# Context loaded a second time in transposed layout, mLSTM values shifted on GpSimd instead of centred on TensorE, router matmuls moved in the step

## The reference

```python
x = x + wkv(w, u, k=layernorm(x), v=ctx)          # a decaying running average of ctx, per channel over time
x = x + attention(layernorm(x))                   # 16 heads of 32
x = x + mlstm(q=layernorm(x), k=ctx, v=ctx)       # 16 heads of 32
x = x + moe(layernorm(x))                         # 32 experts, the best 8 of each token, limited capacity

# in mlstm: ig, fg = [q, k, v] @ Wi, [q, k, v] @ Wf;  D = decay matrix of the gates
Cn = (q @ k.T / sqrt(dh)) * D / normalizer
h  = Cn @ v
hn = (h - h.mean(-1)) * rsqrt(h.var(-1) + eps)    # per head, so a shift of v that is equal over a head's channels drops out
# in moe: probs = softmax(x @ gate_w); top 8; each (expert, token) pair gets a slot while the expert has room
```

## Time and profile before

| what | value |
|---|---|
| time, median of 3 runs | 2157.45 us (2155.42 to 2159.64) |
| profiled execution, first to last instruction | 2155.5 us |
| time of the profiled execution itself | not given apart from the three runs |
| TensorE matmuls busy | 1944.1 us, 90% of the span |
| VectorE busy | 1582.7 us, 73% |
| ScalarE busy | 1203.0 us, 56% |
| GpSimd busy | 1575.2 us, 73% |
| mean granted TensorE clock | 0.977 of full speed |
| first part (pipeline of sequences) | to about 1085 us |

### The profile page before, as it was taken

How to read it: one execution, slowest core, us unless ns; L and a number is a source line. 1 busy time by engine, 2 the same in 40 slices (tenths; PEclk the granted TensorE clock), 3 DMA queues, 4 the chain that set the end, 5 groups by cost and what they waited for, 6 DMA issues and landing times. The chain is left out here.

```text
span 2155.5 us, 66447 instructions
## 1 busy us (share of the span) xinstructions
PE 1944.1 (90%) x22263; PEld 1463.4 (68%) x22296; DVE 1582.7 (73%) x3230; ACT 1203.0 (56%) x3018; POOL 1575.2 (73%) x1776
## 2 busy tenths in 40 slices
PE   0799999999999999997259999999999999999997
PEld 0677667777667766675146777777777777777775
DVE  5688888888888888985236676777766667767664
ACT  3466666666666666665135555555554555545553
POOL 6336778777777777876667777777767777777775
PEclk9999999999999999999579999999999999999999
DMA  3111110111101111101048888777788888887876
GB/s 108 38 34 37 40 39 30 34 34 40 39 29 34 34 39 39 32 27 43 16 111 172 186 193 160 176 181 171 167 178 186 170 178 182 169 190 156 184 153 103
DMA packets 141452, 222.72 MB, mean 103 GB/s; under 512 B 32944, under 2 KB 65840, under 8 KB 141360
## 3 DMA queue, kind: packets, MB, share of 16 engines
q0 software_dynamic: 74752, 144.02, 33.9%
q1 hardware_dynamic: 62000, 69.24, 10.4%
q10 hardware_dynamic: 4608, 8.39, 1.0%
HBM read 136.34 MB, written 96.73 MB: 108 GB/s over the span
## 5 line engine op out<-in xcount | busy, mean ns | idle before, releaser
L2162 POOL DMA_INDIRECT out_dram<-y,m_add x300 | 498.1, 1660 | 171.0 <-POOLq L2170 112.5
L2288 PE MATMUL ps<-xh,wh 128*128 128x256 f16 x1752 | 398.3, 273 | 4.7 <-PEq L2300 4.7
L2289 PE MATMUL ps<-xh,wl 128*128 128x256 f16 x1752 | 398.3, 273 | 0.0
L2154 POOL DMA_INDIRECT xg<-z_scratch,slot_t x292 | 295.8, 1013 | 96.4 <-issue 83.4
L630 POOL DMA_INDIRECT slot_scratch<-pair,slots x256 | 304.8, 1191 | 70.2 <-issue 58.1
L2365 ACT ACTIVATE y<-ps,wts_now 128x512 f32<-128x512 f32 x294 | 185.2, 681 | 143.4 <-ACTq L2364 143.4
L2293 PE MATMUL ps<-xl,wh 128*128 128x256 f16 x1752 | 239.0, 273 | 1.3 <-PEq L2304 1.3
L2439 DVE SCALAR_TENSOR_TENSOR hx<-ps,s 64x256 f16<-64x256 f32 x146 | 62.2, 426 | 216.3 <-DVEq L2462 215.6
L2381 ACT ACTIVATE xh<-ps 128x512 f16<-128x512 f32 x146 | 87.2, 597 | 224.0 <-ACTq L2380 224.0
L2288 PEld LDWEIGHTS ps<-xh,wh 128*128 128x128 f16 x1752 | 171.3, 98 | 45.9 <-issue 12.8
L2289 PEld LDWEIGHTS ps<-xh,wl 128*128 128x128 f16 x1752 | 171.4, 98 | 33.1
(11 more groups left out here) (345 smaller groups left out, 5001.4 us busy)
## 6 DMA issues: line engine op xcount, KB each, us to landing
wst<-in_L_ffn_w_gate_dram SPq DMA_DIRECT2D x32, 384.0 KB
wst<-in_L_ffn_w_up_dram SPq DMA_DIRECT2D x32, 384.0 KB
xt<-in_x_dram SPq DMA_DIRECT2D x32, 256.0 KB
ct<-in_ctx_dram SPq DMA_DIRECT2D x32, 256.0 KB, 2.6
out_dram<-x SPq DMA_DIRECT2D x32, 256.0 KB, 2.1
z_scratch<-zn ACTq DMA_DIRECT2D x32, 256.0 KB, 2.0
wdst<-in_L_ffn_w_down_dram SPq DMA_DIRECT2D x32, 256.0 KB
out_dram<-y,m_add POOLq DMA_INDIRECT x300, 5.1
```

Of the source, the lines that this page charges most:

```text
L2154: pool.indirect_dma_start(out=xg[b][:, h, :], out_offset=None, in_=z_d[:, :], in_offset=bass.IndirectOffsetOnAxis(ap=rows(h), axis=0)).the ...
L2162: pool.indirect_dma_start(out=acc_d[:, :], out_offset=bass.IndirectOffsetOnAxis(ap=m_add[:, k, h:h + 1], axis=0), in_=y[:, k, h, :], in_of ...
L2288: pe.matmul(ps[:, dst, 0:GROUP], wh[:, j, k, c0:c0 + P], xh[:, k, :], start=(k == 0), stop=False)
L2289: pe.matmul(ps[:, dst, 0:GROUP], wl[:, j, k, c0:c0 + P], xh[:, k, :], start=False, stop=False)
```

## The change

The host lays the context out a second time, transposed (`ctx_cols`, channels on partitions). SyncE now makes three context loads per step: `vT` from `ctx_cols` for wkv, `kT2` from `ctx_cols` two steps later for the mLSTM key, and `ct` as before, for the mLSTM values. `ctx_turn`, `vT_copy`, `hold_ctx`, `spread_ctx`, `centre` and `centred_copy` are gone. The values are made by GpSimd from `ct` as each head's 31 columns minus the head's last column (`values`); `bmat` is changed so that `heads_back` takes the mean off and rebuilds the last column. On TensorE `router` moves from behind `heads_back` to ahead of `head_sums`, with its result in another PSUM bank. On VectorE three small operations are written as `scalar_tensor_tensor` with two inputs from SBUF (`stabiliser_floor`, `choose`, `take_places`), and the f32 copy `sel` of the choice is dropped.

```diff
+                def load_own_cols(i):
+                    sp.wait_ge(own_cols_free, 1)
+                    sp.sem_inc(own_cols_free, -1)
+                    sp.dma_start(vT[:, :, :], ctx_cols[bass.ds(i, 1)].rearrange("a p k t -> p (a k) t")).then_inc(own_cols_loaded, 16)
...
                 with sp.Fori(3, nb - 1) as i:
-                    load_ctx(i + 1)
+                    load_key_cols(i - 2)
+                    load_ctx(i - 1)
+                    load_own_cols(i + 1)
                     store(i - 3)
                     load_x(i + 1)
...
-                def spread_ctx():
-                    return pool.tensor_copy(kT2[:, :, :], vTk[:, :, :])
-
-                def hold_ctx():
-                    return pool.tensor_copy(vTk[:, :, :], vT[:, :, :])
+                def values():
+                    heads = ct[:, :].rearrange("p (h d) -> p h d", h=H)
+                    return pool.tensor_tensor(vc[:, :, 0:DH - 1], heads[:, :, 0:DH - 1],
+                                              heads[:, :, DH - 1:DH].to_broadcast([P, H, DH - 1]), ALU.subtract)
...
                         weigh_cc().then_inc(weigh_cc_ready, 1)
                         weigh_gg().then_inc(weigh_gg_ready, 1)
+                    if on(3):
+                        pool.wait_ge(values_free, 1)
+                        pool.sem_inc(values_free, -1)
+                    if on(2):
+                        pool.wait_ge(ctx_loaded, 16)
+                        pool.sem_inc(ctx_loaded, -16)
+                        values().then_inc(values_done, 1)
                     if on(5):
                         pool.wait_ge(pool_step, 1)
                         pool.sem_inc(pool_step, -1)
                         store_pair(3)
                         store_pair(2)
...
-                    if on(0):
-                        vT_copy().then_inc(vT_copy_ready, 1)
...
-                        act.wait_ge(centre_ps, 1)
-                        act.sem_inc(centre_ps, -1)
-                        centred_copy()
...
-                    if on(0):
-                        pe.wait_ge(ctx_loaded, 16)
-                        pe.sem_inc(ctx_loaded, -16)
-                        ctx_turn().then_inc(ctx_turn_ps, 1)
-                    if on(3):
+                    if on(4):
+                        pe.wait_ge(zT_copy_ready, 1)
+                        pe.sem_inc(zT_copy_ready, -1)
+                        router().then_inc(router_ps, 1)
+                    if on(3):
+                        pe.wait_ge(values_ready, 1)
+                        pe.sem_inc(values_ready, -1)
                         pe.wait_ge(decayed_scores0_ready, 1)
                         pe.sem_inc(decayed_scores0_ready, -1)
                         head_sums().then_inc(head_sums_ps, 1)
...
-                    if on(4):
-                        router().then_inc(router_ps, 1)
...
-                        centre().then_inc(centre_ps, 1)
...
-                    return dve.tensor_scalar(fm[:, :], fm[:, :], -50.0, None, ALU.max)
+                    return dve.scalar_tensor_tensor(fm[:, :], fm[:, :], -50.0, fm[:, :], ALU.max, ALU.max)
...
-                    dve.tensor_scalar(sel[:, :], er2[:, :], 0.0, None, ALU.is_lt)
-                    return dve.tensor_scalar(selb[:, :], er2[:, :], 0.0, None, ALU.is_lt)
+                    return dve.scalar_tensor_tensor(selb[:, :], er2[:, :], 0.0, onesf[:, 0:E], ALU.is_lt, ALU.mult)
...
-                    return dve.tensor_tensor(selacc[:, :], selacc[:, :], selb[:, :], ALU.add)
+                    return dve.scalar_tensor_tensor(selacc[:, :], selacc[:, :], 1.0, selb[:, :], ALU.mult, ALU.add)
```

More of the change, by code:

```diff
@@ L255, in build @@
             ctx_loaded = once("ctx_loaded")
+            own_cols_loaded = once("own_cols_loaded")
+            key_cols_loaded = once("key_cols_loaded")
+            own_cols_free = once("own_cols_free")
+            key_cols_free = once("key_cols_free")
+            ctx_free = once("ctx_free")
+            values_free = once("values_free")
+            values_ready = once("values_ready")
+            values_done = once("values_done")
             scratch_set = once("scratch_set")
@@ L504, in _ @@
                   .then_inc(scratch_set, 16)
-                for i in range(1, 3):
-                    load_ctx(i + 1)
-                    load_x(i + 1)
+                load_ctx(0, first=True)
+                load_own_cols(2)
+                load_x(2)
+                load_key_cols(0, first=True)
+                load_ctx(1)
+                load_own_cols(3)
+                load_x(3)
                 with sp.Fori(3, nb - 1) as i:
-                    load_ctx(i + 1)
+                    load_key_cols(i - 2)
+                    load_ctx(i - 1)
+                    load_own_cols(i + 1)
                     store(i - 3)
                     load_x(i + 1)
-                sp.wait_ge(ctx_turn_ps, 1)
-                sp.sem_inc(ctx_turn_ps, -1)
+                load_key_cols(nb - 3)
+                load_ctx(nb - 2)
+                sp.wait_ge(own_cols_free, 1)
+                sp.sem_inc(own_cols_free, -1)
                 store(nb - 4)
@@ L517, in _ @@
                 sp.sem_inc(first_residual_ready_for_sp, -1)
+                load_key_cols(nb - 2)
+                load_ctx(nb - 1)
+                store(nb - 3)
+                load_key_cols(nb - 1)
                 load_weights(sp, 0)
-                for i in range(nb - 3, nb):
+                for i in range(nb - 2, nb):
                     store(i)
@@ L558, in spreads @@
                         put(pick[q_, :, :], 1.0, 0, [[-1, 4], [0, P]])
-                        put(bmat[q_, r, 0:DH - 1], 1.0, 0, [[-1, DH - 1]])
+                        done(pool.memset(bmat[q_, r, 0:DH], -1.0 / DH))
+                        put(bmat[q_, r, 0:DH - 1], 1.0 - 1.0 / DH, 0, [[-1, DH - 1]])
+                        put(bmat[q_, r, 0:DH], 0.0, 1 - DH, [[0, DH]])
                         put(bmat[q_, r, DH:DH + 1], 1.0, 1 - DH, [[0, 1]])
-                        done(pool.memset(bmat[q_, r, DH - 1:DH], -1.0))
-                        put(bmat[q_, r, DH - 1:DH], 0.0, 1 - DH, [[0, 1]])
-                        done(pool.memset(cmat[q_, 32 * r:32 * r + DH - 1], -1.0 / DH))
                 def first_constants():
@@ L715, in step @@
                         pool.sem_inc(qk_ps_for_dve, 1)
[L716 to L724, removed]
+                        pool.sem_inc(key_cols_free, 1)
                     if on(5):
@@ L1250, in project @@
                     return m
-                def ctx_turn():
-                    return turn(CT_BANK, lambda c: ct[:, c * P:(c + 1) * P])
                 def head_sums():
@@ L1304, in gates @@
                                           start=(j == 0), stop=(j == 1))
-                    return m
-                def centre():
-                    for c in range(4):
-                        m = pe.matmul(ps[:, VC_BANK, c * P:(c + 1) * P], kT2[:, c, :], cmat[:, :], start=True, stop=True)
                     return m
@@ L2494, with give @@
     arrays, args = {}, []
-    for name in _INS:
-        a = _np.ascontiguousarray(inputs[name])
+    def give(name, a):
+        a = _np.ascontiguousarray(a)
         arrays[f"in_{name}_dram"] = a
         args.append(nc.dram_tensor(f"in_{name}_dram", a.shape, _mybir.dt.from_np(a.dtype), kind="ExternalInput").ap())
+    for name in _INS:
+        give(name, inputs[name])
+        if name == 'ctx_2048':
+            rows = inputs[name].shape[1]
+            give('ctx_columns', inputs[name].reshape(-1, rows, 4, 128).transpose(0, 3, 2, 1))
     out = nc.dram_tensor("out_0_dram", (32, 128, 512), _mybir.dt.float32, kind="ExternalOutput").ap()
```

65 lines of the change are left out of this document (25 added, 40 removed).

## The result

The changed kernel takes 2196.99 us (median of 4 runs, 2195.15 to 2199.57) against 2157.81 us of the kernel before in the same runs (2155.42 to 2159.64): ratio 1.0184, 95% interval 1.0172 to 1.0195. It is slower by 39.2 us. The forecast was 2184 with a range of 2146 to 2207 and slower as the likeliest sign.

What follows compares the result with a forecast made beforehand. The prediction took a chain through GpSimd, not TensorE, to bound the kernel. Its terms 0.28 + 1.15 - 0.45 = +0.98 us a step over 27 steps gave +26.5 us on 2157.45: 2184 us, range 2146 to 2207.

Steps and rivals of the forecast that it cites:

- the ring: Chain `exp_k`, GpSimd from `weigh_cc` to `spread_sums`, `best_keys`, `o_high`, next `project`: sets the 29.71 us period in 27 steps.
- TensorE is the bound: Rival: 0.53 + 1.0 us of TensorE work come off in each of 32 steps, 2108 us; 3 in 100.
- the whole period: Seven pieces along the chain from `exp_k` to the next step's `exp_k`, said to sum to 29.71 us.
- The way behind `second_residual`: Path by the keys and `best_keys` on VectorE to `o_high`; `selacc` and `sel` said to lie outside, 0 us.
- The router: Router ahead of `head_sums` in place of `ctx_turn` on TensorE: `exp_k` comes 0.28 us later.
- values: New GpSimd operation behind `weigh_gg`, inside the ring: +1.15 us a step (0.62 to 1.3).
- The stores: GpSimd slot stores, beside VectorE's scan `past_weights`: the second loses most of its stretch, -0.45 us together (0 to 0.6).
- More overlaps: Rival: VectorE's `newton_step` or `past_ctx` makes GpSimd wait up to 0.6 us more, +1.6 a step, 2201; 22 in 100.
- Half the loss: Rival: `values` on GpSimd takes only 0.62 to 0.9 us, +0.4 us a step, 2168; 12 in 100.
- centre counted at 0: Removing about 1.0 us of `centre` on TensorE gains 0: `max_turn` waits for `row_max`, idle time takes its place.
- ctx_turn and q: TensorE without `ctx_turn`: `q` waits for `xn_low`, so of 0.53 us saved TensorE keeps 0.11.
- selacc: VectorE's `selacc` comes free as `second_residual` comes 1 us later, saving TensorE up to 0.29 us outside the ring.

Runs made afterwards that it cites:

- u2: Changed kernel with its loop written out and `values` moved on GpSimd ahead of `weigh_cc`: 2170.81 us, ratio 1.0054 to the kernel before.
- u3: Changed kernel, loop written out, `values` ahead of `weigh_cc` and router back behind `heads_back`: 2160.01 us, ratio 1.0004 to the kernel before.
- a4: Kernel before, with the update of `selacc` moved on VectorE into `key_matches`: 2306.40 us against 2308.33, ratio 0.9993.
- r2: Changed kernel written out, router back, two `vc` buffers, `selacc` update in `key_matches`, `best_keys` and `key_matches` behind `divide_by_row_sums`: 2277.95 us, ratio 0.9903 to before.

## Why the prediction came out as it did

**The bound.** Right in the main, and it carried the sign. "What is put into this ring is paid in each of the steps": u2 shows that the same instruction costs 1.16 us a step inside the ring and nothing ahead of it. The case "TensorE is the bound" fell with the result and with u3. Two readings behind it were weaker than they look. The pieces that give "the whole period" would do so along any path. And 29.10 us in step 4 isn't TensorE's own need: that step took 29.60 us in the changed kernel, with less TensorE work, and 28.88 in u3, with the router back, so it follows a chain as well. It holds as an upper bound, which is how it was used.

**The way behind `second_residual`.** Here the path was wrong. The prediction goes by `make_keys` and `best_keys` to `oT`, and says of the three forms that "neither `selacc` nor `sel` is in the ring". `oT` also needs `rinv`, which ScalarE makes from `row_sums` of TensorE, which stands behind `v`, which waits for `selacc`. ScalarE before and after (timeline):

```profile
521.18 0.60 ACT L981 ACTIVATE lsum<-ps 128x512 f32<-128x512 f32 x1 [0.24 <-ACTq L1160]
521.96 0.63 ACT L984 ACTIVATE rinv<-lsum 128x512 f32<-128x512 f32 x1 [0.19 <-ACTq L1163]
```

```profile
538.62 0.60 ACT L993 ACTIVATE lsum<-ps 128x512 f32<-128x512 f32 x1 [0.24 <-ACTq L1164]
539.40 0.63 ACT L996 ACTIVATE rinv<-lsum 128x512 f32<-128x512 f32 x1 [0.19 <-ACTq L1167]
```

`rinv` ends at 522.59 and 540.03, and `oT` starts 0.15 us after it both times. The same 0.15 us lie between `selacc` and `v`, and 0.15 to 0.19 between `row_sums`, `lsum` and `rinv`: no link of this branch has slack, in any looped step between 300 and 900 us. The branch by the keys has a little: `key_matches` (539.78) is followed by `oT` after 0.40 us, where the next operation of the same size (540.79) is followed after 0.33. So the ring goes by `selacc` and `v`, and the keys come 0.07 us earlier (an estimate from these two distances). Both branches start at `second_residual` and the change altered neither, so the sum came out the same by the wrong one: that is luck. It also means that freeing `selacc` would have given 0.07 us, and not the 0.29 of the wait. Farther on `o_high` doesn't release `project` directly either: it ends at 524.25 and `project` starts at 525.72, with `qk`, `z_turn` and the wait for `o_low` between them; which of these carries the ring wasn't taken apart.

**The router.** The mechanism was right, the size of 0.28 us too small: `router` to `head_sums` takes 515.40 - 514.50 = 0.90 us in its new place, so +0.37 us (oT to `weigh_cc`), 0.51 in u2 to u3. In the prediction I had taken 0.81 us, its distance to `q`.

**values.** +1.15 us forecast, 1.02 measured (0.98 from the end of `weigh_gg` to its own): nearer to the 1.04 us of `spread_sums`, which also reads a broadcast input, than to the full 1.27.

**The stores.** This is the term of the sum that was wrong, in size and sign. I took -0.45 us; the chain shows +1.15 - 0.98 = +0.17. I had expected the first store to run free of the scan `past_weights` and the second to meet only its tail. But `own_ctx` wasn't late, so the first begins at 522.19 under `own_ctx` (521.98) and takes 1.45 us instead of 1.11, and the second begins at 523.94 under `weighted_ctx` (L1709, 523.88) and takes 1.45 instead of 1.55: +0.24 us for the two, of which the rest of the chain gives 0.07 back. Without this term the sum is 0.37 + 0.98 = 1.35 us, with it 1.52. The measured 1.52 lies above the forecast's +0.6 to +1.3, in the case "More overlaps" (+1.6 us, 2201), by a different overlap than the one named there. (In "Half the loss" the parts add up to 0.45 to 0.73, not 0.4; nothing hangs on it.)

**centre counted at 0.** Right: 1.01 us of idle time in its place. **ctx_turn and q**: right in kind; `q` even waits 0.19 us.

**selacc.** "It comes free because `second_residual` comes 1 us later" failed. `gv`, ahead of it on VectorE, was held by `scale_heads` (1.81 us), which was late as well, so `selacc` met `second_residual` again and `v` waited 1.31 us. The branch that this holds up is the one above. No run confirms its 0.07 us by taking `selacc` out: a4 and r2, which were made for it, ran with another bound.

**What was to be seen.** Right: `values` at 1.0 us, the idle time ahead of `max_turn`, GpSimd without idle time from `weigh_cc` on. Wrong: the period of 30.4 to 31.1 (31.23), idle VectorE ahead of `best_keys` and more idle TensorE ahead of `z_turn` (the idle time lies ahead of `v`), `own_ctx` at 1.4 us (the small `nrm` ahead of it took the wait). The three VectorE forms alone and `centre` alone weren't tried.

## What to carry to other kernels

A busy share near the top doesn't make an engine the bound: compare a step that has all of its work but lacks another engine's. Then write the ring of a software pipeline link by link, and ask at each whether it starts right behind the end of the one before (0.15 to 0.2 us here), since pieces along any path add up to the period; an operation is dear inside it and free a few rows ahead of it, as far as the wait for the ring's own signal is long enough to hold it (it was in u2, and no longer quite in u3), so when work is moved to another engine its place in that engine's order matters more than its length (31.9 us for a move over two instructions here). Between VectorE and GpSimd a delay doesn't separate two operations that collide if what delays the one holds up the other as well.

## What the runs showed of the hardware that I had not expected

A VectorE operation of 32 elements took 1.50 us and one of 16 elements 0.82 us, by waiting for a GpSimd operation with SBUF inputs; before, the one-input form of the choice took 0.76 us and `selacc`, with two SBUF inputs then too, 1.60. How long a slot store of GpSimd took went with the VectorE operation under which it began (medians between 300 and 900 us): 0.96 us under `row_max`, which reads PSUM; 1.55 (before) under the scan `past_weights` and 1.45 (after) under `own_ctx` or `weighted_ctx`, which have two SBUF inputs; 1.88 and 1.81 under `past_ctx`. Those four kinds ended 0.8 to 1.0 us after that operation did. No run was made to separate the two. And the same kernel took 2159 us at one time and 2300 at another; the traces of the slower runs have TensorE's 32-row f32 matmuls arriving in bursts (3.0 instead of 1.2 us for `qk` in a4) and then, in the step shown, the granted clock at 0.50 for three microseconds. Runs on one and the same chip fell on either side, and the cause of it stays open.
